# Attention on one core: the finish of the first chunk of queries spread over the blocks of the second, and key tiles taken in twos in the two-head layer

## The reference, cut to what matters

```python
# layers 0 and 3: 16 heads of 16
attn = softmax(where(causal, q @ k.T / sqrt(16), -inf)); out = attn @ v      # layer 3: out @ w_out.T + b_out
# layer 1: 8 heads, two maps each, values 32 wide
y = causal_attn(q1, k1, v) - lam * causal_attn(q2, k2, v)
y = (y @ wo.T) * (1 - 0.2)
```

## Time and profile before

| | |
|---|---|
| median of 3 runs | 4897.06 us (4893.74 to 4905.74) |
| profiled execution | 4905.29 us, its span 4903.5 us |
| attention, layer 0, 4 stages | first at 270.3 |
| attention, layer 1, 4 stages | first at 1516.2 |
| attention, layer 3, 4 stages | first at 3733.3 |
| mean granted PE clock | 0.895 |

### The profile page before, as it was taken

One profiled execution on the slowest core, in us unless ns is written; L12 is line 12 of the kernel. 1 busy time (PEld: TensorE's weight loads), 2 busy tenths in 40 slices (PEclk: granted clock), 3 DMA queues, 4 the chain that ended last, 5 costly groups with the idle time before them and its releaser, 6 DMA issues. The chain is left out here.

```text
span 4903.5 us, 61798 instructions
## 1 busy us (share of the span) xinstructions
PE 3872.7 (79%) x22624; PEld 2252.6 (46%) x22624; DVE 2832.8 (58%) x5872; ACT 1821.7 (37%) x2666; POOL 542.5 (11%) x679
## 2 busy tenths in 40 slices
PE   6979879879727868788683777778698798798797
PEld 4525435345212533626343455455474473473573
DVE  5957857659575353543634464454574574664674
ACT  3163171451625444362541233232304415306305
POOL 1001010010010010000000022021231130130230
PEclk9988999989959989989897888789799899899899
DMA  3000000000030000000001000000100000000000
GB/s 85 1 2 1 1 1 1 1 1 1 14 104 1 1 1 1 1 1 1 1 1 50 1 0 0 0 0 0 45 1 6 6 1 5 6 1 5 6 1 10
DMA packets 44815, 45.09 MB, mean 9 GB/s; under 512 B 10320, under 2 KB 40784, under 8 KB 44496
## 3 DMA queue, kind: packets, MB, share of 16 engines
q1 hardware_dynamic: 37424, 31.89, 2.2%
q10 hardware_dynamic: 7072, 9.05, 0.6%
HBM read 36.22 MB, written 4.19 MB: 8 GB/s over the span
## 5 line engine op out<-in xcount | busy, mean ns | idle before, releaser
L596 DVE TENSOR_REDUCE arena<-ps 128x2 f32<-128x1024 f32 (+3 forms) x768 | 699.4, 951 | 74.3 <-PE ps L564 72.5
L760 ACT ACTIVATE arena<-ps 128x1024 f32<-128x1024 f32 (+3 forms) x768 | 568.3, 814 | 69.8 <-PE ps L678 64.2
L834 DVE TENSOR_TENSOR arena<-arena,tri 128x256 f32<-128x256 f32 x512 | 211.4, 424 | 299.7 <-ACT arena L760 293.0
L760 ACT ACTIVATE attention<-ps 128x1024 f32<-128x1024 f32 (+3 forms) x384 | 298.1, 811 | 181.6 <-PE ps L678 181.5
L695 PE MATMUL ps<-arena 128*17 128x512 f32 (+3 forms) x3072 | 333.2, 506 | 3.2 <-DVE arena L834 2.0
L695 PE MATMUL ps<-attention 128*33 128x512 f32 (+3 forms) x1536 | 328.1, 507 | 6.3 <-issue 5.3
L678 PE MATMUL ps<-arena 64*128 64x512 f16 (+3 forms) x1536 | 246.5, 340 | 98.5 <-ACT arena L760 67.7
L1176 PE MATMUL ps<-arena 128*128 128x256 f32 x1152 | 315.7, 404 | 0.6 <-DVE arena L1224 0.3
L1207 ACT ACTIVATE arena<-ps 128x512 f32<-128x512 f32 x144 | 86.0, 597 | 594.4 <-PE ps L1191 594.3
L1761 ACT ACTIVATE arena<-ps 128x256 f32<-128x256 f32 x192 | 63.7, 381 | 615.0 <-PE ps L1703 575.3
L1191 PE MATMUL ps<-arena 128*128 128x512 f32 x576 | 277.3, 606 | 0.0
(11 more groups left out here) (267 smaller groups left out, 6653.3 us busy)
## 6 DMA issues: line engine op xcount, KB each, us to landing
making<-basis SPq DMA_DIRECT2D x16, 768.0 KB, 4.6
out<-x_all SPq DMA_DIRECT2D x8, 512.0 KB, 3.3
arena<-w_down SPq DMA_DIRECT2D x1, 2304.0 KB, 24.8
x_all<-x SPq DMA_DIRECT2D x2, 1024.0 KB, 14.1
x_all<-x ACTq DMA_DIRECT2D x2, 1024.0 KB, 19.8
arena<-arena SPq DMA_DIRECT2D x128, 4.0 KB
making<-w_gate_up SPq DMA_DIRECT2D x1, 2048.0 KB, 15.5
arena<-w_qkv SPq DMA_DIRECT2D x2, 768.0 KB, 6.0
```

The source lines that it names most:

```text
L596: dve.reduce_max(a.mp[:, 2 * j:2 * j + 2, qt, c], out[:, :, 0:w], AX.X).then_inc(self.pair_out, 1)
L760: act.activation(a.p[:, v % ring, :, q0:CH], m.ps[:, b:b + 2, q0:CH], ACT.Exp, scale=HD ** -0.5).then_inc(exped, 1)
L834: dve.tensor_tensor(diag, diag, keep, ALU.min).then_inc(masked, 1)
```

## The change

The work is cut into blocks. In layers 0 and 3 a block is one unit, as before; in layer 1 it is two units, so PE takes score, score, values, values, and the values lag by two blocks, that is four key tiles. The finish of the first chunk is cut into single steps, one each block, in the order turn (in layer 1 turn of half 0, turn of half 1), back, project for tile 0, then tile 1, and so on. It begins at block 19: four blocks in layer 0, twelve in layer 3, sixteen in layer 1. `a.o` has more places (11 for 8 groups, 6 for 4), and a unit's store takes place `unit % places`; only from unit `places` on it waits for the turns. `give` works one half and waits before each for the one before. The last finish keeps its order. Some scratch tiles are left out of layer 1's memory, which does not use them.

```diff
-    ORDER = ((0, 1, 2, 3), (0, 1, 2, 3, 4, 5, 6, 7))
-    units = [(c, g, kt) for c in range(NC) for g in range(groups) for kt in ORDER[c]]
+    units = [(c, g, kt) for c in range(NC) for g in range(groups) for kt in range(TC * (c + 1))]
...
-    second_half = groups * len(ORDER[0])
-    finishing = {second_half + 2 + 2 * i: i for i in range(TC + 2)}
+    per_block = 2 // pairs
+    n_blocks = n_units // per_block
+    places = a.o.shape[1]
+    spaced = [(step, j, half) for j in range(TC) for step, half in
+              [("turn", half) for half in range(halves)] + ([("back", 0), ("project", 0)] if wout is not None else [])]
+    finishing = {groups * TC // per_block + lag + 1 + i: place for i, place in enumerate(spaced)}
+    in_a_row = [(step, k - d) for k in range(TC + 2) for step, d in (("project", 2), ("turn", 0), ("back", 1))
+                if 0 <= k - d < TC and (wout is not None or step == "turn")]
...
-            for n in range(n_units + lag):
-                for j in range(pairs):
-                    if n < n_units:
-                        score(pairs * n + j)
-                    if j == 0 and n >= lag:
-                        values(n - lag)
-                if n in finishing:
-                    finish(0, finishing[n])
+            for block in range(n_blocks + lag):
+                if block < n_blocks:
+                    score(2 * block)
+                    if pairs == 1:
+                        score(2 * block + 1)
+                if block >= lag:
+                    for n in range(per_block):
+                        values(per_block * (block - lag) + n)
+                if block < n_blocks and pairs == 2:
+                    score(2 * block + 1)
+                if block in finishing:
+                    finish(*finishing[block])
...
-            def give(t):
+            def give(t, half):
+                u = halves * t + half
+                if half == 0 and wout is not None and t >= 2:
                     dve.wait_ge(y_turned, t - 1)
-                if t >= 1:
-                    dve.wait_ge(given, halves * t)
-                for half in range(halves):
-                    u = halves * t + half
+                if u >= 1:
+                    dve.wait_ge(given, u)
...
             def store(unit):
-                c, g = divmod(unit, groups)
                 dve.wait_ge(summed, last_of[unit] + 1)
-                if c >= 1:
-                    dve.wait_ge(turned, halves * TC * c)
-                dve.tensor_copy(a.o[:, g, :], m.ps[:, unit % 2, :]).then_inc(evac, 1)
+                if unit >= places:
+                    dve.wait_ge(turned, halves * TC)
+                dve.tensor_copy(a.o[:, unit % places, :], m.ps[:, unit % 2, :]).then_inc(evac, 1)
...
-    a.o = ar.take(groups, CH)
+    a.o = ar.take(groups + groups // 4 + 1, CH)
```

More of the change, by code:

```diff
@@ L698, in values, with turn @@
                 last.then_inc(summed, 1)
-            def turn(t):
+            def turn(t, half):
                 c, j = divmod(t, TC)
+                u = halves * t + half
                 if j == 0:
                     pe.wait_ge(evac, groups * (c + 1))
-                for half in range(halves):
-                    u = halves * t + half
[L706 to L713, removed]
+                if c == 0 and u >= 1:
+                    pe.wait_ge(given, u)
+                if c == 1 and u >= halves * TC + 4:
+                    pe.wait_ge(given, u - 3)
+                for i in range(TC):
+                    group = c * groups + half * TC + i
+                    last = pe.transpose(m.ps[:, turn_bank(u), i * P:(i + 1) * P],
+                                        a.o[:, group % places, j * P:(j + 1) * P], m.ident[:, :])
+                last.then_inc(turned, 1)
             def turn_back(t):
@@ L729, in project, with finish @@
                 last.then_inc(projected, 1)
[L731 to L737, removed]
-            for n in range(n_units + lag):
-                for j in range(pairs):
-                    if n < n_units:
-                        score(pairs * n + j)
-                    if j == 0 and n >= lag:
-                        values(n - lag)
-                if n in finishing:
-                    finish(0, finishing[n])
+            def finish(piece, t, half):
+                if piece == "turn":
+                    turn(t, half)
+                if piece == "back":
+                    turn_back(t)
+                if piece == "project":
+                    project(t)
+            for block in range(n_blocks + lag):
[10 more added lines that the diff above has]
+                    finish(*finishing[block])
             pe.wait_ge(exped, n_units * pairs)
-            for k in range(TC + 2):
-                finish(1, k)
+            for piece, j in in_a_row:
+                for half in range(halves if piece == "turn" else 1):
+                    finish(piece, TC + j, half)
         @block.scalar
@@ L777, in keep_back @@
                 dve.tensor_copy(a.yt[:, t % 2, :], m.ps[:, project_bank(t), 0:D]).then_inc(y_stored, 1)
-            def give(t):
-                if wout is not None and t >= 2:
+            def give(t, half):
+                u = halves * t + half
+                if half == 0 and wout is not None and t >= 2:
                     dve.wait_ge(y_turned, t - 1)
-                if t >= 1:
-                    dve.wait_ge(given, halves * t)
[L784 to L818, removed]
+                if u >= 1:
+                    dve.wait_ge(given, u)
+                sums = m.ps[:, turn_bank(u), :].rearrange("p (h c) -> p h c", c=width)
+                heads = CH // width
+                r = m.small[:, half * heads:(half + 1) * heads]
@@ L820, in store, with finish @@
+            def finish(piece, t, half):
+                if piece == "turn":
+                    give(t, half)
+                if piece == "back":
+                    keep_back(t)
+                if piece == "project":
+                    add(t)
             def store(unit):
-                c, g = divmod(unit, groups)
                 dve.wait_ge(summed, last_of[unit] + 1)
-                if c >= 1:
-                    dve.wait_ge(turned, halves * TC * c)
-                dve.tensor_copy(a.o[:, g, :], m.ps[:, unit % 2, :]).then_inc(evac, 1)
@@ L827, in _ @@
-            for n in range(n_units + lag):
-                if n < n_units and on_diagonal(n):
+                if unit >= places:
+                    dve.wait_ge(turned, halves * TC)
+                dve.tensor_copy(a.o[:, unit % places, :], m.ps[:, unit % 2, :]).then_inc(evac, 1)
+            for block in range(n_blocks + lag):
+                for v in range(2 * block, 2 * block + 2) if block < n_blocks else ():
+                    n = v // pairs
                     q0 = first_query(n)
-                    for j in range(pairs):
-                        v = pairs * n + j
+                    if on_diagonal(n):
@@ L834, in _ @@
                         dve.tensor_tensor(diag, diag, keep, ALU.min).then_inc(masked, 1)
[L835 to L840, removed]
+                for n in range(per_block * (block - lag), per_block * (block - lag + 1)):
+                    if n in last_of:
+                        store(last_of.index(n))
+                if block in finishing:
+                    finish(*finishing[block])
+            for piece, j in in_a_row:
+                for half in range(halves if piece == "turn" else 1):
+                    finish(piece, TC + j, half)
 def attention_memory(m, ar, heads, vd, groups, ring):
     a = Memory()
-    a.o = ar.take(groups, CH)
+    a.o = ar.take(groups + groups // 4 + 1, CH)
     a.y = ar.take(2, D)
@@ L852, in attention_memory @@
     a.v = ar.take(NT, heads, vd + 1)
[L853 to L856, removed]
+    if heads == NM:
+        a.mp = ar.take(4, NT, 2)
+        a.mf = ar.take(4, NT)
+        a.mt = ar.take(2, NT, 8, dtype=F16)
+        a.mrow = ar.take(2, S, dtype=F16)
     base = ar.at
```

22 lines of the change are left out of this document (added).

## The result

The changed kernel takes 4857.15 us (median of 4 runs, 4852.58 to 4857.84) against 4896.05 (4 runs). The two medians differ by 38.9 us; the ratio on record is 0.9909, 95% interval 0.9897 to 0.9921, that is 39 to 50 us less. The profiled execution took 4852.6 us, the lowest of its four.

What follows compares the result with a forecast made beforehand. Layer 1 was bound by PE's work plus finish waits, layers 0 and 3 by ACT for full tiles and PE near the diagonal. From the 4897.1 median, -48.4 - 2.4 + 3.2 = -47.6 us gave 4849.5, range 4826 to 4884.

Steps and rivals of the forecast that it cites:

- The work of PE (seams): Layer 1: same-kind matmuls in a row save 0.11 per score seam and 0.115 per values seam, 10.8 us a batch.
- rival 1: Layer 1: the seams save nothing, since they rest on thin samples; -15 us, 4882; chance 0.12.
- (b): Layer 1, second chunk: an odd tile's score waits for the exponential two before it; +4.8 us a batch.
- Waits that go: Layer 1: 6.5 us of mid-stage finish waits and 1.7 to 1.9 of first-chunk mask waits vanish; 8.4 us a batch.
- (a): Layer 1 start: values begin after six scores, so 2.5 us of waits where there were 1.4; +1.1.
- (d): Layer 1 start: PE's full clock is granted 1 us later; +0.2 us a batch.
- Rival 2: Layer 1: the second chunk's wait on exponentials is not there; -66.8 us, 4830; chance 0.08.
- (c): Layer 1: a turn back comes before its input is ready, waiting 0.1 to 0.2 us four times; +0.5.
- The steps' work "stays on PE": Layer 1: spreading the finish removes its waits, but the work of its steps remains on PE.
- (e): Layer 1's last finish: `give` waits for the first half's subtraction, +0.12 for each of four tiles; +0.5.
- Rival 3: Layer 1: turns wait for DVE anyway, so most of the 6.5 us stays; -22 us, 4875; chance 0.05.
- rival 4: Layer 1, first chunk: the longer start keeps PE at 1.2 GHz, making the kernel slower; +32 us, 4929; chance 0.04.

Runs made afterwards that it cites:

- the run with clumps: Changed kernel with layer 1 still in twos, but its first chunk's finish in six clumps and layers 0 and 3 clumped at the old units: 4885.14 us.
- the mixed order: Changed kernel with layer 1's second chunk taking key tiles in the order 0,4,1,5,2,6,3,7, each pair one full and one diagonal tile: 4831.2 us.

## Why the prediction was right
The forecast was 4849.5 us with -47.6; measured is 4857.15, -39 to -50 by the ratio. The sign, the range and the mechanism held.

- **The work of PE (seams).** Taken 0.11 and 0.115 a seam. The run without seams gives 0.46 for two of each kind, 0.115 each. Right, and rival 1 falls. What makes a change of kind dear (the array's tiling, f16 against f32, the weight loads) no run separates. Rival 1's own price was off: without the seams' 10.8 and with (b) at 3, the sum of -12.1 becomes -3.1 and not -4, 4886 and not 4882.
- **Waits that go.** The 6.5 us went in the changed kernel and stayed in the run with clumps. The mask waits were worth 0.31 a group in seven groups, 2.2 us and not 1.7 to 1.9: the list shows less than they cost.
- **(a) and (d), the start.** Three waits on exponentials before the first values, 1.4, 0.3 and 0.2 us: 1.9 where I had 2.5, so +0.5 and not +1.1. The full clock came 7.6 us after the first score (1521.16), against 6.7 before and 7.7 forecast, as this window of the changed kernel shows (0.61 of a us means 0.78 at half clock, so it rose at 1528.78). In the same way the 0.66 of the earlier trace rows puts layer 3's rise at 3741.7, 8.4 us after its first score and not 8:

```profile
1528.00:1529.00 1.00, 1.00 (x10) 0.16 (x6) 0.00 (x0) 0.00 (x0) 0.00 (x0) 0.61 0.00 0
```

- **(b)** is the step that carried most and was right: undisturbed groups 8.82 (forecast 8.8 to 8.9), and 8.23 when the order takes the wait away. Rival 2 falls.
- **(c)** 0.17 four times, 0.7 for 0.5.
- **The steps' work "stays on PE"**: the term that was mis-sized, by less than it seems. A step alone stands between two changes of kind: a turn costs 0.59 and not 0.49, a turn back 0.37 and not 0.31, a projection 1.06 and not 0.97. That is 10.4 us a stage for the 16 steps, where these prices of the forecast give 9.0. But the clumps already paid most of it: their turns before a wait took 0.60 to 0.66, their last projections 1.06 and 1.13, all 16 steps 10.0. (The groups say the same: 22.9 + 11.3, less two of 8.84 and 6.5 of waits, is 10.0.) Spreading made the steps dearer by 0.5 us a stage. Groups with finish are 11.05, not 10.8.
- **(e)** 0.12 was forecast and 0.11 is there in the timeline. Its price of 0.5 holds: 0.5 and 0.6 where last finishes at the same granted clock are compared.
- **Layer 1 in sum**: -12.1 forecast, -12.5 measured. The start was 0.6 and the masks 0.4 better than forecast, the lone steps 0.5 and (c) 0.2 worse; that gives -12.4.
- **Layer 3**: -0.6 forecast, -0.5 measured. **Layer 0**: +0.8 and +1.0, and the run with the old places shows that the places are the cause. Rival 3 falls with the waits; rival 4 with the granted clock of 0.87 in the first chunk.
- **The sum**: -48.4 - 2.4 + 3.2 against -50.2 - 2.1 + 4.7 by the stages of the two profiles: -47.6 both. That they agree to 0.1 is luck, since layer 1 gained 1.8 more and layer 0 lost 1.5 more than forecast. What is off is the last step, that the shift of the profile carries to the median: it was +8.2 in the forecast, and the changed kernel's profile lay 4.6 us below its median. In the ten profiles here (before, changed, eight runs) the untouched rest of the kernel took between 3610 and 3621 us. For layer 3 one cause is shown, the clock that an earlier arrival meets. In the two kernels' profiles themselves nothing is given back (the rest is 5 us shorter in the changed one), so which stage makes its median less good than its profile is open.

## What to carry to other kernels
Where an in-order engine alternates two kinds of work, count the changes of kind as a cost of their own, and look at which pair each block puts together: pairing long with short work kept both engines fed (8.82 to 8.23 us a group) where pairs in natural order gave all of it back as a wait. Fill-in work is free only beside tiles where the engine that carries it waits; next to others it costs its full time, and standing alone a little more than in a clump (10.4 us for 10.0 here). Price the clump by all its steps, since the cheapest line of it is not its mean. And judge an edit of some us by stage lengths in the profile, since executions differ by 5 to 10 us in places that it never touched.

## What the runs showed that I had not expected
- A gain can vanish in the clock of a later stage: layer 3's batches stay 355 us apart with an attention stage of 97.0 or 95.4 us.
- Waits can hide inside merged lines: the mixed order's PE shows no wait at all in 23 us, yet two scores of 0.48 together take 0.74.
- The two halves of the change are worth 5.1 and 4.0 us a stage alone, 12.5 together.
